# Message stage of a graph network on one NeuronCore: one small matmul less in each PSUM bank

## The reference, cut to what matters

```python
xg0, xg1 = y0[edge_src], y1[edge_src]          # 64 scalars, 64 vectors of 3, of each edge's source
mid0 = w_a * xg0 * ea0                         # ea0, ea1: one scalar, one vector of 3 per edge
mid1 = w_b * einsum('euc,ec->eu', xg1, ea1) * INV_SQRT3
mid2 = (w_c * xg0)[:, :, None] * ea1[:, None, :]
mid3 = (w_d * ea0)[:, :, None] * xg1
mids = concatenate([mid0, mid1, mid2, mid3], axis=1)        # 8 components of 64
agg  = segment_sum(mids, edge_dst, num_segments=n)          # sum over the edges of each node
```

## Time and profile before

| | us |
|---|---|
| median of 3 runs | 2243.17 (2240.6 to 2246.63) |
| the profiled execution, own time | 2247.85 |
| its span in the trace | 2246.1 |
| message stage, first PE product to last addition | 1188.9 to 1787.9 |
| PE busy over the span | 1915.6 (85%) |
| mean granted clock of PE | 0.911 |

### The profile page before, as it was taken

How to read it: one execution, slowest core, us unless ns; L and a number is a source line. 1 busy time by engine, 2 the same in 40 slices (tenths; PEclk the granted TensorE clock), 3 DMA queues, 4 the chain that set the end, 5 groups by cost and what they waited for, 6 DMA issues and landing times. The chain is left out here.

```text
span 2246.1 us, 40254 instructions
## 1 busy us (share of the span) xinstructions
PE 1915.6 (85%) x10789; PEld 1526.5 (68%) x10789; DVE 1155.0 (51%) x2768; ACT 1035.6 (46%) x3210; POOL 1010.4 (45%) x1048
## 2 busy tenths in 40 slices
PE   2799999997597649999358999999999888949998
PEld 1566666664365539999236888888888776639997
DVE  6333333333223664444658888888888641031111
ACT  3454444442145213333356666666666446413332
POOL 2677777777200025554017777777772000012221
PEclk7899999999797569999678999999999989969999
DMA  9677777776200349999526777777775231056663
GB/s 233 190 235 229 234 238 227 235 236 183 59 0 1 95 129 351 352 354 312 131 79 193 208 209 207 208 209 208 208 207 146 58 71 41 23 163 194 193 203 93
DMA packets 268760, 401.12 MB, mean 179 GB/s; under 512 B 65997, under 2 KB 160835, under 8 KB 268316
## 3 DMA queue, kind: packets, MB, share of 16 engines
q1 hardware_dynamic: 217928, 258.46, 37.4%
q0 software_dynamic: 50176, 137.57, 21.2%
q10 hardware_dynamic: 462, 2.76, 0.5%
HBM read 311.83 MB, written 87.84 MB: 178 GB/s over the span
## 5 line engine op out<-in xcount | busy, mean ns | idle before, releaser
L1770 POOL DMA_INDIRECT msg_got<-y_dram,block_src x416 | 406.4, 977 | 228.6 <-issue 124.6
L1787 ACT ACTIVATE msg_scaled<-msg_plain,msg_w 128x125 f32<-128x125 f32 x1392 | 415.9, 386 | 192.6 <-DVE msg_plain L1820 182.2
L651 POOL DMA_INDIRECT sum_got<-xn_dram,block_src x416 | 393.5, 946 | 137.9 <-issue 112.7
L1811 PEld LDWEIGHTS msg_ps_z<-msg_prod,msg_scaled 128*125 128x125 f32 x2784 | 341.7, 188 | 13.2
L1811 PE MATMUL msg_ps_z<-msg_prod,msg_scaled 128*125 128x128 f32 x2784 | 343.1, 273 | 0.0
L1805 PE MATMUL msg_ps_z<-msg_prod,msg_plain 128*125 128x256 f32 x928 | 300.7, 406 | 17.3 <-DVE msg_prod L1839 17.3
L1286 ACT ACTIVATE ffn_run_hid<-ffn_run_ps_h,cols 128x128 f32<-128x128 f32 x512 | 146.0, 368 | 345.9 <-PE ffn_run_ps_h L1245 345.9
L697 PEld LDWEIGHTS sum_ps_sum<-sum_got,sum_onehot 128*125 128x125 f32 x928 | 177.1, 196 | 188.0 <-issue 172.6
L697 PE MATMUL sum_ps_sum<-sum_got,sum_onehot 128*125 x928 | 255.8, 400 | 49.0 <-POOLq L645 48.3
L1343 POOL DMA_INDIRECT ffn_run_rows<-ffn_rows,ffn_token x96 | 99.0, 1031 | 357.5 <-POOLq L72 328.8
L757 DVE TENSOR_TENSOR agg<-sum_ps_sum,agg 125x256 f32 x232 | 98.5, 425 | 313.5 <-PE sum_ps_sum L697 311.2
(11 more groups left out here) (305 smaller groups left out, 2174.4 us busy)
## 6 DMA issues: line engine op xcount, KB each, us to landing
ffn_run_w<-in_L_ffn_w SPq DMA_DIRECT2D x128, 512.0 KB, 6.6
msg_w<-edge_w SPq DMA_DIRECT2D x232, 260.0 KB, 3.5
edge_w<-sum_wide SPq DMA_DIRECT2D x52, 1040.0 KB, 4.9
ffn_run_w<-in_L_ffn_Wd SPq DMA_DIRECT2D x32, 1024.0 KB, 5.7
sum_got<-xn_dram,block_src POOLq DMA_INDIRECT x416, 3.4
msg_got<-y_dram,block_src POOLq DMA_INDIRECT x416, 3.7
ffn_rows<-xn SPq DMA_DIRECT2D x10, 560.0 KB
table_got<-ffn_results SPq DMA_DIRECT2D x10, 560.0 KB
```

What stands on the lines that cost most here:

```text
L651: pool.indirect_dma_start(got[:, (b + 1) % RING, u, :], None, k.xn_dram, bass.IndirectOffsetOnAxis(ap=k.block_src[:, b, u:u + 1].bitcast(U ...
L1770: pool.indirect_dma_start(got[:, (b + 1) % RING, u, :, :].rearrange("p k v -> p (k v)"), None, k.y_dram, bass.IndirectOffsetOnAxis(ap=k.bl ...
L1787: last = act.activation(scaled[s % MB][:, x, c, :], plain[s % MB][:, c, :], ACT.Copy, scale=w[:, s % RS, c, D + x:D + x + 1])
L1811: last = pe.matmul(z[0:P, 4:6 + x:1 + x, :], by[:, x, c, :], p[:, c, 4 + x:8:3 - x, :], start=False, stop=(x == 2 and u == KC - 1))
```

## The change

The zero matmul of line 1807 goes, with the row of zeros, its semaphore `zeros_made`, PE's wait for it and DVE's memset of 64 words. The other matmuls keep their order, sizes and marks; `skip_group_check` is added to them, which is an argument for the program that builds the kernel and not an instruction.

```diff
-        zeros, zeros_made = ph.sb("zeros", [1, 2 * MUL], BF16), ph.sem("zeros_made")
...
-            pe.wait_ge(zeros_made, 1)
...
-                        pe.matmul(z[0:P, 0:4, :], mask[:, c, :], p[:, c, 0:4, :], start=(u == 0), stop=False)
-                        if u == 0:
-                            pe.matmul(z[0:P, 6:8, :].rearrange("p k v -> p (k v)"), k.ones[0:1, 0:P], zeros[0:1, :], start=False, stop=False)
+                        pe.matmul(z[0:P, 0:4, :], mask[:, c, :], p[:, c, 0:4, :], start=(u == 0), stop=False, skip_group_check=True)
...
-                                             start=False, stop=(x == 2 and u == KC - 1))
+                                             start=False, stop=(x == 2 and u == KC - 1), skip_group_check=True)
...
-            dve.memset(zeros[:, :], 0.0).then_inc(zeros_made, 1)
```

## The result

The changed kernel takes 2185.0 us (median of 4 runs, 2180.4 to 2186.7), the kernel before 2243.9 in the same series: 58.9 us less, a ratio of 0.9735 with a 95% interval of 0.9714 to 0.9756. The forecast was 2179, in a range of 2170 to 2199. The profiled execution took 2180.36, with a span of 2178.6.

A forecast was written before the change was run, and what follows sets the result against it. PE was taken to bound the message stage, with DVE next. Head -0.8, middle 112 steps x 0.537 = -60.1 and tail -3.2 gave -64.1, so 2243.2 became 2179 us, range 2170 to 2199.

The forecast's parts named there:

- PE was the bound: Message stage before the change: PE, busy without a gap, alone sets the step of 5.13 us; POOL follows.
- 0.39 us per bank go, 0.20 of them at the seams: PE's banks: without the zero matmul 2.17 us instead of 2.56, as both wide pairs then run without loss.
- The rival of the seams that stay: PE's banks: only 0.19 us goes per bank, step 4.74 us, 2198; PE still bound wholly or partly: chance 0.13.
- DVE becomes the bound at 4.59: Message stage after the change: DVE's step of 4.59 us exceeds PE's 4.35, gaining 0.54 us per step; chance 0.75.
- POOL holds with a microsecond or two of margin, 1.25 us per gather: Message-stage gathers: 4.48 us per step on average; per tile a draw of 2.0 us against 2.5 given back.
- the rival: POOL becomes the bound: DVE's two-SBUF-input products slow gathers, some 3 us lost, 2182; stretched further, near 2205, chance 0.05.
- Register loads hidden: DVE's stream in the message stage: register loads run beside its instructions, end no gap and cost nothing.
- Tail 13.8 us: Message stage, last mask to end of last additions: 13.8 us instead of 17.03, a gain of 3.2.
- Head -0.8: PE's first message step, partly at 1.2 GHz: 6.75 us instead of 7.53, so 0.8 less.
- The clock rival: PE's idle 5% of each step lowers the granted clock; at 0.80 the step is 5.44 us, 2279; chance 0.03.
- From stage to whole time: Stages behind the message stage: same instructions, 64 us earlier; clock-change moments may shift this 3 us either way.

## Why the prediction was right, step by step

*PE was the bound.* Right: 0.26 us more on DVE changed nothing before.

*0.39 us per bank go, 0.20 of them at the seams.* Right in size, 2.174 us per bank measured. I had taken the matmul's being odd for the cause and left open in what; it is the single row. The rival of the seams that stay, and with it the rule of the Trainium skill on overlapping weight loads that I set against the rows ("TensorE: Matmul & The Clock Gate", The mechanism), does not hold here: full-row loads hide behind full-row matmuls, 0.109 and 0.215 us per record, and it is beside the one-row matmul that they do not. I had quoted the rule short: the same section also lets a load be pulled ahead when it goes to the background weight buffer. That would fit the full-row stream, but no run here shows where a load goes.

*DVE becomes the bound at 4.59.* Right: 4.57, and it answers to added work by all of it.

*POOL holds with a microsecond or two of margin, 1.25 us per gather.* Wrong, and with it the reading that it rests on, that POOL waited for the products before. It did not: its idle time before a gather stayed at 0.30 us, and the 1.282 us came from gathers that DVE's products made longer. The prediction argued against the rival that contention has no reason to keep an exact lock to PE's step; it did keep one, with one longer gather in each step. What a wait for the products looks like is seen in the run with the f32 zero matmul from one row, whose step of 5.55 us is long enough for POOL to get that far ahead:

```profile
1401.02 0.94 POOL L1770 DMA_INDIRECT msg_got<-y_dram,block_src  x1 [0.72 <-DVE msg_prod L1839]
```

That PE was the bound stays true; the first step above shows it without this reading. After the change the gathers take 1.302 on average, so a step draws 1.793 x 2 x 1.302 = 4.67 us of gathers on average, above DVE's 4.57; the lead shrinks all through the stage. The rival named the mechanism and about its price, 3 us, and I gave it too little room. The sum hid it: 2.5 us of longer steps and 0.65 in the tail, against 0.02 us per step (2.4 us) that DVE was faster than I had it.

*Register loads hidden.* Right in the plain step. In a step that waits for a block they come out behind the wait: after the step of 1.07 us of sequencer wait at 1568.5, the addition started 0.38 us late.

*Tail 13.8 us.* Measured 1717.77 - 1703.32 = 14.45 from the last mask, 0.65 more. The last products waited for the last block (1705.11 issued, used at 1708.42), but that is some 0.2 of it: with products from PSUM nothing waits there, and the tail is 14.25. Another 0.35 lies in the last two additions, which take 1717.77 - 1715.89 = 1.88 us and not 1.53, because the second starts 0.50 us after the first has ended. The last 0.1 I can't place.

*Head -0.8.* From the first PE product to the first waiting mask 7.74 us before and 1189.03 - 1182.00 = 7.03 now: -0.7.

*The clock rival.* Did not occur: the granted clock reads 1.00 from 1200 to 1700, with PE waiting some 0.2 us per step.

*From stage to whole time.* 63.2 us in the stage, 58.9 by the medians, with an interval of 55 to 64. The difference lies within it; I have no other cause for it.

## What to carry to other kernels

Look for seams before you count matmuls: where start-to-start distances around a matmul exceed those of its neighbours, the cost is in how it differs from them. A bias or zero product from one row, put between full-row f32 products, cost 0.39 us here; the same from 128 rows cost 0.11, and none at all when another engine was the bound. Before calling an engine a follower because it keeps the bound's pace, look at where its time goes: a wait shows in the idle time before its instructions (0.72 us), contention in their own duration (1.05 for 0.95). Here three engines stood within 8% (PE 4.35, DVE 4.57, POOL 4.67), so that removing work from one was worth at most the distance to the next.

## What the runs showed of the hardware that was not expected

- A one-row f32 zero matmul of 128 columns, two records, adds 0.603 us to a bank, against 0.218 for the same over 128 rows.
- A bf16 matmul over full rows between f32 ones starts 0.056 us ahead of the next and delays the second record behind it by 0.053.
- DVE products with two SBUF inputs stretched 53 of 416 gathers by some 0.3 us each after the change; with one input in PSUM none was. Before the change 100 were longer, by some 0.1 us each, one in each step.
- One chip had gathers at 1.46 us on average in the neighbour sum and the whole kernel 15% slower (2589 against 2244), with the durations of gathers, PE and DVE instructions themselves unchanged.
